# The second attention's first quarter laced into the tail of the first attention

## The reference

```python
# L0: attention over channels, x and ctx seen as (8, 128 channels, 256 tokens), 16 heads of 8
q, k, v = Wq @ x + bq, Wk @ ctx + bk, Wv @ ctx + bv
attn = softmax(q^T k / sqrt(8))
mean, ex2 = attn @ v, attn @ (v * v)
std = sqrt(relu(ex2 - mean * mean))
x = (instance_norm(x) * std + mean) * mask
# L1: every sequence attends to [ctx, x] (256 keys), 16 heads of 16
q = x @ q_w + q_b;  kv = concat([ctx, x]) @ kv_w + kv_b
h = softmax(mask(q k^T / 16)) @ v @ out_w + out_b + x
x = x + gelu(rmsnorm(h) @ w1 + b1) @ w2 + b2
# L2: two cross attentions (16 heads of 128) and an MLP;  L3: one attention and an MLP
```

## Time and profile before

| | us |
|---|---|
| three runs, median (lowest to highest) | 1260.13 (1251.97 to 1260.76) |
| profiled execution, its own time | 1252.72 |
| its span | 1250.9 |
| PE busy | 1109.2 (89%) |
| DVE busy | 746.2 (60%) |
| ACT busy | 723.7 (58%) |
| POOL busy | 320.7 (26%) |

### The profile page before, as it was taken

One profiled execution on the slowest core, in us unless ns is written; L12 is line 12 of the kernel. 1 busy time (PEld: TensorE's weight loads), 2 busy tenths in 40 slices (PEclk: granted clock), 3 DMA queues, 4 the chain that ended last, 5 costly groups with the idle time before them and its releaser, 6 DMA issues. The chain is left out here.

```text
span 1250.9 us, 23776 instructions
## 1 busy us (share of the span) xinstructions
PE 1109.2 (89%) x8224; PEld 960.1 (77%) x8224; DVE 746.2 (60%) x1761; ACT 723.7 (58%) x2096; POOL 320.7 (26%) x433
## 2 busy tenths in 40 slices
PE   3899995999978989999999899999998696899687
PEld 3677774667758879999998789999997695676486
DVE  4777774677776535555556735555555847455653
ACT  1577774777764356666665555666665423777531
POOL 5234344555430002111111122111111202332210
PEclk9899997999988999999999989999998897799899
DMA  6111101000002101111111011111101101000101
GB/s 197 25 29 53 34 23 34 2 2 1 1 31 81 43 26 43 43 43 43 43 64 43 1 43 43 43 43 43 43 35 35 51 2 34 2 2 1 34 1 35
DMA packets 20364, 43.65 MB, mean 35 GB/s; under 512 B 3347, under 2 KB 10773, under 8 KB 20246
## 3 DMA queue, kind: packets, MB, share of 16 engines
q1 hardware_dynamic: 20246, 42.12, 10.1%
HBM read 36.87 MB, written 1.05 MB: 30 GB/s over the span
## 5 line engine op out<-in xcount | busy, mean ns | idle before, releaser
L1601 POOL TENSOR_TENSOR pt<-pt,prec 128x256 f32<-128x256 f32 (+1 forms) x224 | 179.8, 803 | 669.2 <-DVE prec L1445 514.0
L604 PE MATMUL ps<-rs 128*128 128x256 f32 x480 | 147.2, 307 | 29.7 <-DVE rs L1480 19.6
L1109 ACT ACTIVATE pt<-ps,nmax 128x129 f32<-128x129 f32 x256 | 92.1, 366 | 96.7 <-DVE nmax L1437 95.9
L1244 DVE TENSOR_TENSOR rs<-wraw,rs 128x256 fp32r<-128x256 f32 (+2 forms) x108 | 69.2, 644 | 122.9 <-ACT rs L986 122.1
L605 PE MATMUL ps<-rs 128*128 128x256 f32 x480 | 139.3, 290 | 0.0
L606 PE MATMUL ps<-rs 128*128 128x256 f32 x480 | 139.3, 290 | 0.0
L1060 ACT ACTIVATE pt<-ps,nmax 128x256 f32<-128x256 f32 (+1 forms) x256 | 104.9, 421 | 48.0 <-DVE nmax L1383 30.0
L604 PE MATMUL ps<-ht,rs 128*128 128x256 f32 (+1 forms) x368 | 127.5, 346 | 1.0 <-ACT fs L1147 1.0
L604 PEld LDWEIGHTS ps<-rs 128*128 128x128 f32 x480 | 95.5, 199 | 36.0 <-DVE rs L1480 12.7
L605 PE MATMUL ps<-ht,rs 128*128 128x256 f32 (+1 forms) x368 | 121.2, 329 | 0.0
L606 PE MATMUL ps<-ht,rs 128*128 128x256 f32 (+1 forms) x368 | 120.9, 328 | 0.0
(11 more groups left out here) (196 smaller groups left out, 3009.5 us busy)
## 6 DMA issues: line engine op xcount, KB each, us to landing
wraw<-in_packs SPq DMA_DIRECT2D x55, 512.0 KB, 3.4
bvr<-in_l2rows SPq DMA_DIRECT2D x16, 256.0 KB, 4.5
rs<-rs SPq DMA_DIRECT2D x80, 32.0 KB, 1.9
ht<-rs SPq DMA_DIRECT2D x48, 32.0 KB, 1.9
row<-in_rows SPq DMA_DIRECT2D x2, 640.0 KB, 4.8
out<-X SPq DMA_DIRECT2D x1, 1024.0 KB, 5.0
X<-in_x SPq DMA_DIRECT2D x1, 768.0 KB, 8.4
XH<-in_ctx SPq DMA_DIRECT2D x1, 768.0 KB, 10.2
```

The costliest lines, as they stand in the source:

```text
L604: nc.tensor.matmul(dst, w[0], m[1], start=start, stop=False)
L1109: last = nc.scalar.activation(prob[:, g % 3, k * D:k * D + P + 1], ps[:, S_BANK + g % 2, k * D:k * D + P + 1], ACT.Exp, bias=nmax[:, g % 4 ...
L1244: last = nc.vector.tensor_tensor(dst[1], src, f32(dst[0]), ALU.subtract)
L1601: nc.gpsimd.tensor_tensor(pr, pr, prec[:, u % 4, 0:nh].unsqueeze(2).broadcast_to([P, nh, keys]), ALU.mult)\
```

## The change

L0 and L1 become one list, `first_order()`. A pair's result is finished as soon as its two sequences are done: the event `fin` is split into `dev` (the square root, now of four sequences at once), `mul` and `res`, and pairs 0 and 1 go, with their `nT lat`, to ticks 88 to 100 of L0. L1's selection weights are taken at ticks 118 and 120. L1's projections and stacks of the first pair stand at ticks 125 to 145, and its units from tick 134 on, one for two ticks; L0's units end at tick 127 (`S`) and 136 (`X`). Pairs 2 and 3 are finished between L1's units 6 and 10. The zeroing of the key stacks is split in halves (`zk`), the values' is `zv`. L0's key blocks and L1's `prob`, `probT` lie elsewhere so that both stages can live at once, and the first L1 users of a shared bank or tile wait for L0's last use.

```diff
-    for k in range(3):
-        put(L0_UNITS + L0_LAG + 8 + k, "fin", k)
+    put(118, "w", "L1sel0")
+    put(120, "w", "L1sel1")
+    for k, (dev, mul, res, lat) in enumerate([(88, 92, 94, 96), (None, 96, 98, 100), (147, 148, 149, 150), (None, 150, 152, 153)]):
+        if dev:
+            put(dev, "dev", k // 2)
+        put(mul, "mul", k)
+        put(res, "res", k)
+        put(lat, "nT", "lat", k)
+    put(131, "zk", 0)
+    put(135, "zk", 1)
+    put(141, "zv", 0)
...
+    for tick, e in zip((125, 126, 128, 144, 145, 129, 132, 133), head, strict=True):
+        put(tick, *e, st="L1")
+    for u, events in enumerate(units):
+        for e in events:
+            put(L1_START + 2 * u, *e, st="L1")
...
-        prob, probT = pt[:, 0:3, :], pt[:, 3:6, :]
+        prob, probT = pt[:, 8:11, :], pt[:, 5:8, :]
...
+        kb2 = sb("kb2", [P, 2, 4, D], F32R)
...
-        kbd = [kb3[:, i, :, :] for i in range(3)] + [kb2[:, i, :, :] for i in range(2)]
+        kbd = [kb2[:, i, :, :] for i in range(2)] + [kb3[:, i, :, :] for i in range(3)]
... (PE: first S, T, PV of L1)
+                    elif ph == "L1":
+                        pe.wait_ge(Z["mx"], L0_UNITS)
...
+                    elif ph == "L1":
+                        pe.wait_ge(Z["ex"], L0_UNITS)
...
+                        elif ph == "L1" and im == 0:
+                            pe.wait_ge(Z["pv"], L0_STEPS // 2)
... (ACT)
-                            act.wait_ge(g_setup, {"L1": 2, "L3": 3}[ph])
+                        act.wait_ge(g_setup, 2 + i if ph == "L1" else 4)
...
-                    elif e == "fin":
-                        act.wait_ge(l0var, 2 * i + 2)
-                        nc.scalar.activation(ms[:, 1, 2 * i:2 * i + 2, :], ms[:, 1, 2 * i:2 * i + 2, :], ACT.Sqrt).then_inc(l0dev, 1)
+                elif e == "dev":
+                    act.wait_ge(l0var, 4 * i + 4)
+                    dev = ms[:, 1, 4 * i:4 * i + 4, :]
+                    nc.scalar.activation(dev, dev, ACT.Sqrt).then_inc(l0dev, 1)
... (POOL)
-                        if ph == "L1" and 1 <= i <= B:
-                            add_row(XH, "L1o", i - 1)
+                    if ph == "L1" and i in (4, 14):
+                        pool.wait_ge(Z["vd"], B)
+                        pool.wait_ge(fin, 4 if i == 4 else 8)
+                    if ph == "L1" and (4 <= i < 8 or 14 <= i < 18):
+                        add_row(XH, "L1o", i - 4 if i < 8 else i - 10)
...
-                        if i == 2:
+                elif e == "zk":
+                    if i == 0:
+                        pool.wait_ge(Z["sm"], L0_UNITS)
+                        pool.wait_ge(Z["s2"], L0_STEPS)
+                    else:
                             pool.wait_ge(Z["xm"], L0_UNITS)
-                            zero_keys("L1")
-                        if i == 3:
+                    nc.gpsimd.memset(ksA[:, i, :].bitcast(F32), 0.0).then_inc(g_setup, 1)
+                elif e == "zv":
+                    pool.wait_ge(Z["oeA"], B)
                             zero_values()
```

More of the change, by code:

```diff
@@ L88 @@
 L0_PTS = 12
+L1_START = 134
 LATE = {"L1": ("dq", "dk", "w", "nT"),
@@ L956, in _ @@
[L956 to L962 removed]
+                if e[0] in ("nS", "nX", "nT"):
+                    norm_step(*e)
+                elif e[0] == "k":
+                    wide([e])
+                elif e[0] == "up":
+                    _, c, f2 = e
+                    if c == 0 and f2 == 0:
+                        taken(pe, name + "w1_0")
+                        taken(pe, name + "w1_1")
+                    pe.wait_ge(nrm["lo"], c + 1)
+                    bank = j_bank()
+                    for fi in range(2):
+                        f = 2 * f2 + fi
+                        for k in range(KT):
+                            last = three(bank[:, fi * D:(fi + 1) * D], both(lambda i: mw1[name][i][:, k, f * P:(f + 1) * P]),
+                                         both(lambda i: ht[i][:, k, 2 * c:2 * c + 2, :]), k == 0, k == KT - 1)
+                    j_full(last, (m["gelu"], (FT // 2) * c + f2 + 1))
+                elif e[0] == "down":
+                    c = e[1]
+                    if c == 0:
+                        taken(pe, name + "w2_0")
+                        taken(pe, name + "w2_1")
+                    pe.wait_ge(m["lo"], (FT // 2) * (c + 1))
+                    bank = j_bank()
+                    for b in range(2):
+                        for f in range(FT):
+                            last = three(bank[:, b * D:(b + 1) * D], both(lambda i: gg[i][:, (FT * c + f) % GT, b * P:(b + 1) * P]),
+                                         both(lambda i: mw2[name][i][:, f, :]), f == 0, f == FT - 1)
+                    j_full(last, (m["out"], c + 1))
@@ L1202, in _ @@
+            for st, *e in first_order():
+                l0(*e) if st == "L0" else att(st, *e)
+            for e in mlp_order("L1"):
+                mlp("L1", ACT.Gelu_apprx_tanh, e)
             act.wait_ge(M["L1m"]["out"], B // 2)
```

1104 lines of the change are left out of this document (540 added, 564 removed).

## The result

The changed kernel takes 1267.64 us (median of 7 runs, 1263.01 to 1270.44), the kernel before in the same session 1260.13. The ratio, which is estimated from all the runs, is 1.0066 with a 95% interval of 1.0038 to 1.0094 (the two medians lie 7.5 us apart). So it is slower, by 8.3 us in 1260; measured a second time (12 runs) the ratio was 1.0046 (1.0015 to 1.0077), 5.8 us. Four single executions further down (one of a repeat of before, two of `e1`, one of `e2`) took 1571 to 3535 us, and all ratios leave them out. I had forecast 1.4 us faster; 1267.64 lies in the range, but the sign is wrong. The profiled execution of the changed kernel has a span of 1264.3 us and a time of its own of 1266.11; the span of before was 1250.9.

What follows compares the result with a forecast made beforehand. PE's own list was taken to set the pace in L0 and L1's attention. Terms -10.2 + 2.9 + 3.6 + 0.6 + 1.7 = -1.4 us, against the runs' median of 1260.13, gave 1258.7, stated as 1258, range 1244 to 1271.

Steps and rivals of the forecast that it cites:

- L0, forecast +7.1: Inside L0: early root +2.9, results and transposes of pairs 0 and 1 +3.6, L1's selection +0.6 us.
- dev0: Early root at tick 88: a 3.6 us block on ACT delays the Exp that PV9 needs, +2.9 us, bounds 1.9 and 3.6.
- the slow rival: The rival the clock stays down, on the slower side: some +10 us, 1270; chance 0.12.
- The pairs 0 and 1 with the selection: In L0, DVE's work for both pairs makes PE wait, +3.6 us; L1's selection on DVE adds +0.6.
- The head, forecast -8.5 with the clock: L1's start up to S10: the earlier start gains 10.2 us, half clock around PV15 costs 1.7.
- Some 3.4 us at half clock with PV15 in them: Behind the 3.1 us wait before PV15, PE's clock halves and PV15 doubles: +1.7 us, bounds 0 and 6.
- `res3` 232.6, `nT3`, and S10 at 233.0: End of L1's head: `nT3` follows `res3` and S10 goes at 233.0, where before it went at 243.22.
- The first term: L1's earlier start, compared S10 with S10: -10.2 us; bounds a lead of 16 or of 4.
- the clock stays down: From PV9's wait, and from 201 to S10, PE's short pieces run at half clock: some +10 us, 1270; chance 0.12.
- slack in L0 takes the insertions: In L0, idle ACT and DVE time absorbs the insertions, costing some 2 in place of 7.1: -11.5 us, 1248.6; chance 0.28.
- The fourth rival: L1's S0 goes early but `zv` or `mul3` come as late as before: first term 0, 1267; chance 0.08.
- The table switch: Rival on ACT: each switch costs as much again as its load, +1.2 us, 1261; chance 0.06.

Runs made afterwards that it cites:

- e1: The changed kernel with the early root moved from tick 88 to the head of tick 90, under PV9; ratio to before 1.0016.
- e2: The changed kernel with L1's units, root and late pairs one tick later, so step 1's `pk` copy follows the Exp of X127; ratio to before 1.0032.
- e6b: The changed kernel with matmuls nobody reads put into PE's waits, those of pairs 2 and 3 ahead of the shared bank's wait; ratio to before 1.0019.
- e12: The changed kernel with `res3` on DVE behind unit 9's maximum, its reciprocal and `pk`'s copy; ratio to before 1.0015.
- e10: The changed kernel with the edits of e8 and e2 together; 1256.4 us, ratio to before 0.9961.
- e8: The changed kernel with `dev0`, `res0` and `res1` moved to the PVs of ticks 90, 98 and 106; ratio to before 0.9996.
- e4: The changed kernel with the root, results and transposes of pairs 2 and 3 put 4 to 9 ticks later; ratio to before 1.0031.
- e13: e10 with the edit of e12 added; median 1250.87 us, ratio to before 0.9951.
- e7: The kernel before with only the new places of tiles, no instruction moved; ratio to before 0.9994.

## Why the prediction was wrong, step by step

Worked out were -10.2 + 2.9 + 3.6 + 0.6 + 1.7 = -1.4. Measured from PV8 to S10: 117.95 for 111.89, +6.1. From S10 on the two are alike, as said (117.5 and 117.2 us to the last score). The miss is 7.5 us, and it has two places.

**L0, forecast +7.1, measured +9.2** (6.87 + 2.33 from the table). `dev0`: 2.9 forecast, 3.25 by `e1`. The block was right to 0.1; the work behind the wait at half clock, 1.4 here and 0 to 2.4 in other profiles, I had put down to the slow rival alone, and the place of the root without it costs 1.9. The pairs 0 and 1 with the selection: 4.2 forecast, 9.2 - 3.25 = 5.95 measured. The two waits that I had named are in PE's list at `nT0` (1.13) and `pp` (0.68), with more at the second pair; what the selection costs by itself no run shows. The mechanism was right, the size too low by 1.75 and inside its bounds.

**The head, forecast -8.5 with the clock (-10.2 + 1.7), measured -3.1.** This is where it failed. From PV13 to S10 before took 66.6 us and after 63.5. S0 came where I had it: 195.8 and the 13.15 by which the clock of the trace had by then moved (4.0 and 9.2) are 208.95. The waits before PV15 (3.03 for 3.1), `dv0` behind `zv`, and `nT2` (4.01 for 5.3) were there too. Two steps were wrong, of 2.3 and 3.1 us:

- "Some 3.4 us at half clock with PV15 in them: its 1.93 us doubles, and the chain to `zv` goes through it", +1.7 us. S0 to S8 was forecast at 30.1, and 31.8 with this term; it took 34.1. In `e6b`, with the clock at 1.00, it took 30.6: the chain was right to half a microsecond, and the clock cost 3.5 where I had 1.7 (2.6 in the second profile of the changed kernel). PV15 itself cost the 1.7 that I had given it. What I had put at nothing was the work behind PV15, and the second fall of the clock behind the wait before `dv1`, which my sum doesn't name.
- "`res3` 232.6, `nT3`, and S10 at 233.0." S8 to S10 was forecast at 7.1 and took 10.2. I followed POOL and DVE to `res3`, and that part held: `res3` ends 7.1 behind S8 (forecast 6.7). What I didn't follow is what `res3` holds up on DVE: unit 9's maximum, and with it an Exp, ACT's copies and the bank that `nT3` itself needs. `nT3` comes 2.65 behind the end of `res3` (250.16 to 252.81) and not at once. In `e12` it follows at once, but `res3` itself ends 8.1 behind S8, as it now stands behind `pk`'s copy: 1.6 of the 3.1 are won back, and the other 1.5 are that place and the slightly longer chain to `mul3`.

The sentence "The wait before `nT2` will cost the clock too, but behind it PE has 1.9 us to spare before `nT3`: nothing" held in effect. The clock was at 0.50 from 242 to 248, and S8, its PV and `pq` ran slow; but S8 to S10 waits for POOL and DVE, and takes 10.08 at full clock (`e6b`).

The first term's bounds (-16 to -4) just missed -3.1 with the clock and held it without (-3.1 less 3.6, which `e6b` wins from S0 to S10, is -6.7).

The rival that describes much of what happened is the third: **the clock stays down**, with a sum of some +10. I gave it 0.12. It was right in mechanism and in its places up to S8, and too dear: it had +1.7 behind PV9 (measured 1.37) and +7 beyond the forecast's own 1.7 from PV15 to S10 (measured some 1.9 to 2.0, as `e6b` wins 3.6 there). Of the miss of 7.5 us the clock that I hadn't priced is some 3.2, the stretch around `res3` 3.1; the results of pairs 0 and 1 are 1.75 and the chain up to S8 0.5, less 1.0 by which the root's place was too dear. Its point of decision was set by "more than a quarter of the loose part's work is slow"; in the profile after, from PV15 to S10, six slices of 2 us stand at 0.50 (216 to 220, 232 to 234, 242 to 248). I had seen 0.72 in the loose stretch of before and a clock of 0.50 behind one wait, and priced only one of four waits by it.

The rival "slack in L0 takes the insertions" (0.28) is refuted: L0 became 9.2 longer. The fourth rival, that the new start isn't early in effect, was nearer in its time (1267) than in its reason: S0 stood 29.2 earlier behind PV13 than before, and S10 still 3.1 earlier, where that rival had 0; but most of the lead was gone. The table switch costs its loads and its root, and no more (142.48 to 146.15). The prediction also said that a difference under 1% can't be told from none; 0.66% was, with an interval of 0.28% to each side.

What `e10` shows beside this: the early start of L1 does pay. The place of three early steps took 4.9 us in L0 (6.5 to the last score), and starting L1 one tick too soon 4.3.

## What to carry to other kernels

Moving work into the gaps of a dense stage puts new waits into a list whose engine is the bound; place each inserted instruction under the engine's longest piece of work (here a PV of 1.93 us), and much of its cost goes: `e8` won 4.9 of the 9.2 us that L0 had lost. Where PE's work behind a wait is what the rest waits for, price the wait twice, once for itself and once for that work at half clock; where another engine's chain sets the pace behind it, once. And when a waiting instruction is put ahead of others on an engine, follow what stands behind it until the chain ends, since it may lead back to what the waiting step itself needs.

## What the runs showed of the hardware

- Behind most waits of PE of 3 to 4 us the clock was at 0.50 for some 3 to 7 us, and PV's 32 matmuls took 3.30 to 3.64 in place of 1.93; once, behind 3.0 us, it stayed at 1.00 (`e4`, PV9). Behind shorter waits it was either: 1.57 us with the fall (before `dv1` in the changed kernel) and 1.58 without (the same wait in `e8`), 2.4 without (`e10`, `nT3` at 237.8), 1.88 with (`e13`). The instructions of before lost the clock at 232 in one execution (`e7`) and kept it in another.
- Matmuls in the waits held it at 1.00 in all slices from 140 to 262 (`e6b`), and won 3.5 us where PE's work was waited for (S0 to S8) and 0.1 where it wasn't (S8 to S10).
- A load of ACT's table took 1.28 us and began as the Exp before it ended; Exp to Exp over two loads and a root of 1.06 us took 3.67 (142.48 to 146.15).
- The timed runs of the kernel before spread from 1250 to 1266 us; on two of the four chips of the study (the sessions of `e1` and `e12`) with a gap of 2 to 4 us in the middle, on the other two without. The longest runs have a mean granted clock of some 0.94 and the shortest one of 0.95. Differences under some 4 us (0.3%) are not told apart by 10 runs.
